# Half of the feature-spreading DMAs of a linear-attention stage issued by GpSimd instead of SyncE, with the output-bias adds queued behind them

## The chip, the cores and the metric

The kernel runs on one core of a Trainium2 chip. Its engines are TensorE (PE), VectorE (DVE), ScalarE (ACT), GpSimd (POOL) and SyncE (SP); each works through a queue of its own in order, and they meet only at semaphores. The metric is the device time of one execution in microseconds. A change of 0.2% is 4.6 us here.

## The reference

Two transformer layers in a row over 2048 tokens of width 512. The change sits in the attention of the first one, a linear attention that mixes only the 16 heads of a token with one another:

```python
q = (x @ Wq.T + bq); k = (x @ Wk.T + bk); v = (x @ Wv.T + bv)      # 16, 8, 8 heads of 32
q, k = rope(q), rope(k)
qp = sin_cos(q / |q| @ R.T);  kp = sin_cos(k / |k| @ R.T)           # 32 features per head
kv  = einsum('bhsf,bhsd->bsfd', kp, v)                              # per token, over heads
out = einsum('bhsf,bsfd->bhsd', qp, kv)
x = x + out @ Wo.T + bo
```

Before and after it stand routed spline layers, and behind those the second layer: a gated feed-forward, a differential attention and another feed-forward.

## The kernel before

Everything is written by hand, with one semaphore for each kind of step. The 2048 tokens are four chunks of 512. The attention stage runs from 230 to 705 us of the profiled execution as five rounds, `i` = -1, 0, 1, 2, 3. In round `i` each engine works on several chunks at once: `new` = i + 1 is projected and turned into features, `now` = i gets its scores, its weighted sums and its output product, `look` = i + 2 is prepared, and `back` = i - 1 is routed for the next layer. The order of each engine's queue is the order in which `b_tensor`, `b_scalar`, `b_vector`, `b_pool` and `b_sync` write it.

The features of `new` leave VectorE as six blocks `f_hi`/`f_lo` of [128, 512] in 16 bits: two of keys, then four of queries. VectorE writes the last piece of block z at L1647, semaphore `b_f_lo`. A block holds its heads along the partitions; the score product wants a head's high and low parts stacked in 96 partitions. So the blocks are copied within SBUF by DMAs, three batches for each chunk: the **keys** into `ks` once two blocks stand, the **first queries** into `qs` once four stand, the **second queries** once all six stand. Each batch is 12 DMAs, three parts by four quarters `j` of the partitions, each 32 partitions by two rows of 512, 64 KB. All are issued on SyncE's queue, `spread` at L1568. Between the first and the second queries that queue also writes the values to HBM and reads them back rearranged (L1580, one DMA; L1584, eight DMAs that wait until the write has landed).

Who waits for them: ScalarE regroups the keys at L1486 (`keys`, first in the queue ahead of the rest of the features' turns) and waits for `b_ks`; TensorE's first score product of the next round, L1298, waits for `b_qs`, that is for all 24 query DMAs:

```python
pe.wait_ge(s["b_qs"], 384 * (now + 1))     # L1289, at y == 0 of a round
e.wait_ge(s["b_ks"], 192 * (new + 1))      # L1485, ahead of keys(0)
```

GpSimd has two jobs in a round. It multiplies by the cosines (L1547) and squares (L1550) for the six blocks of `new`; and it adds the output bias to the four tiles of `now` (L1555), each as soon as VectorE has added the product to the residual (L1655, `b_res`). The statistics that VectorE takes of these tiles at step 2 of the next round (L377) wait for `b_bo`.

Of the kernel before, what the change touches and what calls it, by code (L numbers as in the profile page):

```python
# [28 lines left out]
NCH = NTOK // CH  # L29
# [61 lines left out]
ap_oh ap_turned ap_oht ap_rows ap_read  # L91
n_var n_ln n_std n_norm n_h n_turned n_hi n_lo
b_v_done b_v_in b_v_out b_vr b_qk_done b_qf b_cos b_rot b_rope b_sq b_nsum b_n2 b_ln b_n b_r b_proj b_p b_spread b_y
b_reduced b_feat b_f_hi b_f_lo b_ks b_ksg b_qs b_s b_mask b_pv b_ot_hi b_ot_lo b_out b_res b_bo
f_gate f_up f_th f_tmp f_prod f_hi f_lo f_down f_out
c_in c_h c_turned c_ct_hi c_ct_lo c_w_hi c_w_lo c_lam_in c_lam_dot c_lam_exp c_mask c_set c_qk_done c_qk c_qk_hi c_qk_lo c_v_done c_v_hi c_v_lo
c_score c_max c_negmax c_max_turned c_maxt c_scored c_exp c_p_hi c_p_lo c_av c_ev c_on c_u c_sq c_msum c_ms c_lnm c_rms
# [1099 lines left out]
PAIRS = CH // GROUP // 2  # L1197
# [22 lines left out]
def need(eng, sem, value):  # L1220

    if value > 0:
        eng.wait_ge(sem, value)


def b_roles(i):


    return [n if 0 <= n < NCH else None for n in (i, i + 1, i + 2, i - 1)]
# [49 lines left out]
def b_tensor(k, pe, i):  # L1279

    s = k.s
    now, new, look, back = b_roles(i)
# [4 lines left out]
    def score(y):  # L1287
        if y == 0:
            if now:  # L1289
                pe.wait_ge(s["b_res"], TPC * now)  # L1290
            pe.wait_ge(s["b_v_in"], TPC * (now + 1))
            pe.wait_ge(s["b_qs"], 384 * (now + 1))
        if y % 4 == 0:
            pe.wait_ge(s["b_ksg"], 4 * now + y // 4 + 1)
        need(pe, s["b_mask"], PAIRS * now + y - 1)
        for q in range(2):
            toks = slice((2 * y + q) * GROUP, (2 * y + q + 1) * GROUP)
            ins = pe.matmul(k.ps[:, SCORE_BANK[y % 2], 256 * q:256 * q + 256].rearrange("p (h t) -> p h t", h=16),  # L1298
                            k.ksg[0:96, 2 * y + q, :], k.qs[0:96, :, toks], start=True, stop=True)
        ins.then_inc(s["b_s"], 1)  # L1300
# [135 lines left out]
def grouped(ref):  # L1436

    return ref.rearrange("p a (h g) -> p a h g", g=32)  # L1440
# [5 lines left out]
def b_scalar(k, e, i):  # L1446

    s = k.s
    now, new, look, back = b_roles(i)
    route = 1 + NCH  # L1450

    def sums(g):
        e.wait_ge(s["b_pv"], PAIRS * now + 4 * g + 4)
        e.activation(grouped(k.ot_hi)[:, :, :, 8 * g:8 * g + 8],
                     k.ps[:, SUM_BANK, :].rearrange("p (a h g) -> p a h g", g=8, a=4),
                     ACT.Copy, scale=O_SCALE).then_inc(s["b_ot_hi"], 1)

    def projected(t):
        e.wait_ge(s["b_qk_done"], 6 * new + t + 1)
        e.activation(k.qf[:, t, :], k.ps[:, PROJ_BANK[t % 2], :], ACT.Identity, bias=k.bqk[:, ORDER[t]:ORDER[t] + 1],  # L1460
                     scale=1.0 / (W_SCALE * A_SCALE)).then_inc(s["b_qf"], 1)

    def inverse():
        e.wait_ge(s["b_n2"], new + 1)
        e.activation(k.nr[0:24, 1, :], k.nr[0:24, 0, :], ACT.Ln).then_inc(s["b_ln"], 1)
        e.wait_ge(s["b_ln"], new + 1)
        e.activation(k.nr[0:24, 1, :], k.nr[0:24, 1, :], ACT.Exp, scale=-0.5).then_inc(s["b_n"], 1)

    def turns(z):
        if new is None:  # L1470
            return
        e.wait_ge(s["b_p"], 6 * new + z + 1)
        need(e, s["b_reduced"], 6 * new + z - 1)
        e.activation(k.turns[:, z % 2, :], k.ps[:, WIDE_BANK, :], ACT.Copy).then_inc(s["b_spread"], 1)
        e.wait_ge(s["b_reduced"], 6 * new + z + 1)
        e.activation(k.ang[:, z % 2, :], k.ang[:, z % 2, :], ACT.Sin, bias=k.c["phase2pi"], scale=-float(2 * np.pi))\
            .then_inc(s["b_feat"], 1)
        e.wait_ge(s["b_feat"], 6 * new + z + 1)
        e.activation(k.f_hi[:, z, :], k.ang[:, z % 2, :], ACT.Copy, scale=A_SCALE).then_inc(s["b_f_hi"], 1)

    def keys(g):
        if new is None:
            return
        if g == 0:
            e.wait_ge(s["b_ks"], 192 * (new + 1))  # L1485
        e.activation(k.ksg[0:96, 8 * g:8 * g + 8, :].rearrange("p g (h t) -> p g h t", h=8),  # L1486
                     k.ks[0:96, :, P * g:P * g + P].rearrange("p h (g t) -> p g h t", t=GROUP), ACT.Copy)\
            .then_inc(s["b_ksg"], 1)

    if i == NCH - 1:  # L1490
        use_log(e)
    for y in range(PAIRS + 1):
        if now is not None and y and y % 4 == 0:
            sums(y // 4 - 1)
        if new is not None:
            if y in QK_AT:
                projected(QK_AT.index(y))
            if y == SPREAD_AT + 1:
                inverse()
        if look is not None and y == LOOK_START + 1:  # L1500
            apply_scalar(k, e, look, 1, LOOK_BANK)
        if back is not None:
            if y == 3:
                token_root_scalar(k, e, back, 1)
            if y == 5:
                token_root_scalar(k, e, back, 2)
            if y == 7:
                token_write_scalar(k, e, back)
        if i == NCH - 1:
            if y in (8, 9):  # L1510
                route_sign_scalar(k, e, back, route, 2 * y - 16, LAST_BANK)
                route_sign_scalar(k, e, back, route, 2 * y - 15, LAST_BANK)
            if y == 12:
                route_hot_scalar(k, e, back, route, LAST_BANK[0])

    body = back is not None and new is not None
    for z in range(4):
        turns(z)
    keys(0)
    keys(1)  # L1520
    turns(4)
    keys(2)
    keys(3)
    turns(5)
    if look is not None:
        use_log(e)
        norm_root_scalar(k, e, look)
        norm_write_scalar(k, e, look, look, k.h, range(TPC), s["n_h"])
    if body:
        for c in range(KC):  # L1530
            route_sign_scalar(k, e, back, route, c, BACK_BANK)
    if look is not None:
        for c in range(KC):
            turn_scalar(k, e, look, c, NEXT_TURN[c])
    if body:
        route_hot_scalar(k, e, back, route, BACK_BANK[0])


def b_pool(k, e, i):
    s = k.s  # L1540
    now, new, look, back = b_roles(i)
    if new is not None:
        for z in range(6):
            e.wait_ge(s["b_qf"], 6 * new + z + 1)
            if z == 0:
                need(e, s["b_proj"], 6 * new)
            e.tensor_tensor(k.qr[:, z, :], k.qf[:, z, :], k.c["cos"], ALU.mult).then_inc(s["b_cos"], 1)  # L1547
            e.wait_ge(s["b_rope"], 6 * new + z + 1)
            need(e, s["b_nsum"], 6 * new + z - 1)
            e.tensor_tensor(k.q2[:, z % 2, :], k.qr[:, z, :], k.qr[:, z, :], ALU.mult).then_inc(s["b_sq"], 1)  # L1550
    if now is not None:
        for u in range(TPC):
            e.wait_ge(s["b_res"], TPC * now + u + 1)
            xt = k.x[:, now * TPC + u, :]
            e.tensor_tensor(xt, xt, k.bo, ALU.add).then_inc(s["b_bo"], 1)  # L1555


def b_sync(k, sp, i):


    s, scratch = k.s, k.d["values"]
    f = (k.f_hi, k.f_lo)

    def spread(stack, parts, blocks, heads, sem):
        for part in range(3):
            for j in range(4):
                dst = stack[32 * part:32 * part + 32].rearrange("p (b j) t -> p j b t", j=4)[:, j, heads]
                sp.dma_start(dst, f[parts[part]][32 * j:32 * j + 32, blocks, :]).then_inc(sem, 16)  # L1568

    if i == 0:  # L1570
        sp.wait_ge(s["ug_out"], 16 * NCH)
    sp.wait_ge(s["b_f_lo"], 6 * i + 2)
    need(sp, s["b_ksg"], 4 * i)
    spread(k.ks, (0, 0, 1), slice(0, 2), slice(0, 2), s["b_ks"])
    sp.wait_ge(s["b_f_lo"], 6 * i + 4)
    need(sp, s["b_s"], PAIRS * i)
    spread(k.qs, (0, 1, 0), slice(2, 4), slice(0, 2), s["b_qs"])
    sp.wait_ge(s["b_v_in"], TPC * (i + 1))
    need(sp, s["b_vr"], 128 * i)
    sp.dma_start(scratch.rearrange("(u p) n -> p u n", p=P), k.v0).then_inc(s["b_v_out"], 16)  # L1580
    sp.wait_ge(s["b_v_out"], 16 * (i + 1))
    need(sp, s["b_pv"], PAIRS * i)
    for h in range(8):
        sp.dma_start(k.vr[GROUP * h:GROUP * h + GROUP], scratch[:, 32 * h:32 * h + 32]  # L1584
                     .rearrange("(g t) d -> t g d", t=GROUP)).then_inc(s["b_vr"], 16)
    sp.wait_ge(s["b_f_lo"], 6 * i + 6)
    spread(k.qs, (0, 1, 0), slice(4, 6), slice(2, 4), s["b_qs"])


def b_vector(k, V, i):  # L1590
# [456 lines left out]
def use_log(e):  # L2047

    e.preload_act_table_set("natural_log_exp_and_others")
# [858 lines left out]
```

## Time and profile before

| | |
|---|---|
| median of 3 runs | 2310.25 us (2309.74 to 2310.73) |
| the profiled execution | 2309.18 us |
| its span, first to last instruction | 2307.3 us |
| busy: PE, DVE, ACT, POOL | 2010.7, 1267.2, 727.0, 220.6 us |
| 16 DMA engines' mean busy share | about a fifth |

Busy times are sums over the whole span, and stages differ: in the second layer TensorE is nearly always busy, in the attention stage it waits for others now and then. What a transfer costs there is seen only from the instruction that waits for it.

### The profile page before, as it was taken

How to read it: one execution, taken by the hardware profiler on the slowest of the kernel's cores; microseconds unless marked ns; L12 is line 12 of the kernel's file. 1: busy time of each engine (PE TensorE's matmuls, PEld its weight loads, DVE VectorE, ACT ScalarE, POOL GpSimd, SP SyncE). 2: the span in 40 equal slices, each digit the busy share in tenths (PEclk: the TensorE clock that was granted, in tenths of full speed). 3: DMA queues.
4: the chain of work that ended last, by engine and by line, in shares of the span. 5: the costliest groups of instructions: out<-in, count | busy, mean ns of one | idle time of the engine just before them, and what ended most of it. 6: DMA issues, size and time to landing. Idle time of an engine off the chain costs nothing. (4 is left out here: it accounts for less than half of the span.)

```text
span 2307.3 us, 29065 instructions
## 1 busy us (share of the span) xinstructions
PE 2010.7 (87%) x11854; PEld 945.0 (41%) x11854; DVE 1267.2 (55%) x2323; ACT 727.0 (32%) x1131; POOL 220.6 (10%) x164
## 2 busy tenths in 40 slices
PE   4784868887864899999998999989998999999998
PEld 3442323333332444444443444444444444444443
DVE  5777447576566455554565356625574466623322
ACT  4562132333321222232243223522343223412211
POOL 3630201201100000001000100001000100000000
PEclk7986878878865899999999999999999999999999
DMA  7224030302123122212111111111111111132321
GB/s 257 92 74 171 0 60 13 48 19 42 37 51 120 64 93 100 93 54 73 46 56 46 56 46 46 57 55 43 41 65 37 64 47 56 56 101 101 112 102 60
DMA packets 91136, 158.71 MB, mean 69 GB/s; under 512 B 44342, under 2 KB 55932, under 8 KB 86268
## 3 DMA queue, kind: packets, MB, share of 16 engines
q1 hardware_dynamic: 91004, 156.86, 21.4%
q8 instruction: 94, 1.54, 0.3%
q14 instruction: 38, 0.31, 0.0%
HBM read 128.52 MB, written 18.87 MB: 64 GB/s over the span
## 5 line engine op out<-in xcount | busy, mean ns | idle before, releaser
L1184 PE MATMUL ps<-arena 128*128 128x512 f16 (+1 forms) x4512 | 1021.8, 382 | 19.8 <-DVE arena L1965 12.9
L1184 PEld LDWEIGHTS ps<-arena 128*128 128x128 f16 x4512 | 437.4, 99 | 544.2 <-issue 57.1
L1910 PE MATMUL ps<-arena 128*128 128x512 f16 x1536 | 349.1, 383 | 29.5 <-DVE arena L1956 16.2
L1910 PEld LDWEIGHTS ps<-arena 128*128 128x128 f16 x1536 | 147.4, 98 | 207.4 <-issue 29.4
L1965 DVE SCALAR_TENSOR_TENSOR arena<-arena,ps 128x512 f32<-128x512 f32 x128 | 87.8, 686 | 210.1 <-ACT arena L1932 209.5
L1932 ACT ACTIVATE arena<-ps,arena 128x512 f32<-128x512 f32 x128 | 87.6, 684 | 362.3 <-PE ps L1184 362.1
L2517 ACT ACTIVATE arena<-ps 128x1024 f32<-128x1024 f32 (+3 forms) x128 | 90.1, 704 | 254.6 <-PE ps L2426 254.5
L2622 DVE CAST arena<-arena 128x1024 f16<-128x1024 f32 (+3 forms) x128 | 66.2, 517 | 150.6 <-ACT arena L2517 148.6
L2588 DVE TENSOR_REDUCE arena<-ps 128x2 f32<-128x256 f32 (+3 forms) x128 | 99.5, 819 | 65.1 <-PE ps L2370 65.1
L1993 DVE SCALAR_TENSOR_TENSOR arena<-ps,arena 128x512 f32<-128x512 f32 x64 | 44.0, 687 | 139.6 <-PE ps L1910 139.4
L1974 DVE SCALAR_TENSOR_TENSOR arena<-ps,arena 128x512 f32<-128x512 f32 x128 | 95.7, 748 | 39.3 <-PE ps L1184 39.1
L2624 DVE TENSOR_TENSOR arena<-arena 128x1024 f16<-128x1024 f32 (+3 forms) x128 | 111.4, 870 | 4.4
L2568 POOL TENSOR_TENSOR arena<-arena 128x512 f16<-128x512 f32 x32 | 37.1, 1159 | 643.8 <-ACT arena L2495 643.8
L1956 DVE TENSOR_TENSOR arena<-arena 128x512 f16<-128x512 f32 x128 | 90.8, 710 | 4.0 <-ACT arena L1924 4.0
L1924 ACT ACTIVATE arena<-arena 128x512 f16<-128x512 f32 x128 | 79.7, 622 | 17.5 <-DVE arena L1974 17.5
L1599 DVE TENSOR_TENSOR arena<-ps,arena 128x256 f32<-128x256 f32 x128 | 47.9, 417 | 67.3 <-PE ps L1298 66.6
L1827 PE MATMUL ps<-arena 128*128 128x128 f32 x192 | 32.5, 325 | 54.7 <-ACT arena L2042 54.7
L2572 POOL TENSOR_TENSOR arena<-arena 128x512 f32<-128x512 f32 x16 | 19.0, 1186 | 581.5 <-DVE arena L2635 581.5
L2424 PE MATMUL ps<-arena 32*128 32x512 f16 (+3 forms) x768 | 72.9, 293 | 0.0
L731 PE MATMUL ps<-arena 128*128 128x128 f32 x240 | 45.6, 336 | 30.5 <-DVE arena L968 17.7
L2492 ACT ACTIVATE arena<-ps 128x512 f32<-128x512 f32 x32 | 19.1, 597 | 166.7 <-PE ps L1184 166.7
L1311 PE MATMUL ps<-arena 128*32 128x64 f32 x1024 | 42.0, 295 | 26.7 <-DVE arena L1607 14.0
(267 smaller groups left out, 2394.8 us busy)
## 6 DMA issues: line engine op xcount, KB each, us to landing
arena<-wug_dram SPq DMA_DIRECT2D x128, 512.0 KB, 3.3
arena<-wd_hi_dram SPq DMA_DIRECT2D x16, 1024.0 KB, 5.0
arena<-wd_lo_dram SPq DMA_DIRECT2D x16, 1024.0 KB, 7.2
arena<-arena SPq DMA_DIRECT2D x144, 64.0 KB, 2.1
wug_dram<-arena SPq DMA_DIRECT2D x4, 2048.0 KB, 15.8
arena<-_attn_hidden_states_dram SPq DMA_DIRECT2D x4, 1024.0 KB, 11.9
arena<-in_L_ffn_W_up_dram SPq DMA_DIRECT2D x8, 512.0 KB, 4.8
arena<-in_L_ffn_W_down_dram SPq DMA_DIRECT2D x4, 1024.0 KB, 7.3
```

Of the source, the lines that this page charges most:

```text
L1184: ins = pe.matmul(out, left[a](c), right[b](c), start=(at == 0), stop=(at == 3 * n - 1))
L1910: ins = pe.matmul(k.ps[:, bank, :], act[x][:, slot, cols], wd[y][:, f, :], start=(f == 0 and m == 0), stop=(f == 7 and m == 2))
L1924: e.activation(k.act_hi[:, g % ACT_SLOTS, :], k.prod[:, g % 2, :], ACT.Copy).then_inc(s["f_hi"], 1)
L1932: e.activation(k.th[:, g % 2, :], k.ps[:, GATE_BANK, :], ACT.Tanh, scale=k.wscale[:, FB + a:FB + a + 1])\
L1956: e.tensor_tensor(k.act_lo[:, g % ACT_SLOTS, :], k.prod[:, g % 2, :], k.act_hi[:, g % ACT_SLOTS, :], ALU.subtract)\
L1965: e.scalar_tensor_tensor(out=th, in0=th, scalar=1.0, in1=k.ps[:, GATE_BANK, :], op0=ALU.add, op1=ALU.mult)\
L1974: e.scalar_tensor_tensor(out=k.prod[:, g % 2, :], in0=k.ps[:, UP_HALF_BANK, :], scalar=k.wscale[:, a:a + 1], in1=th, op0=ALU.mult, op1=ALU ...
L2424: pe.matmul(k.ps[:, bank, queries], x[rows, 4 + b, keys], y[rows, b, queries], start=False, stop=False)
L2517: e.activation(k.p32[:, t % 2, :, queries], k.ps[:, 0:2, queries], ACT.Exp, scale=SCORE).then_inc(s["c_exp"], 1)
L2588: e.tensor_reduce(k.mx[:, u, 4 * b + 2 * j:4 * b + 2 * j + 2], k.ps[:, bank:bank + 2, 0:(u + 1) * P], AXX, ALU.max).then_inc(s["c_max"], 1)
L2622: e.tensor_copy(k.p_hi[:, t % 2, :, queries], k.p32[:, t % 2, :, queries]).then_inc(s["c_p_hi"], 1)
L2624: e.tensor_tensor(k.p_lo[:, t % 2, :, queries], k.p32[:, t % 2, :, queries], k.p_hi[:, t % 2, :, queries], ALU.subtract).then_inc(s["c_p_l ...
```

## The change

The loop over the four quarters is split. SyncE keeps quarters 0 and 1 of every batch, six DMAs; GpSimd issues quarters 2 and 3, six DMAs of the same shape, on semaphores of their own (`b_ks2`, `b_qs2`). On GpSimd all three batches stand behind the six cosine/square pairs of `new` and ahead of the four bias adds of `now`. TensorE and ScalarE wait for both semaphores.

```diff
+            pe.wait_ge(s["b_qs"], 192 * (now + 1))
+            pe.wait_ge(s["b_qs2"], 192 * (now + 1))
-            pe.wait_ge(s["b_qs"], 384 * (now + 1))
...
-            e.wait_ge(s["b_ks"], 192 * (new + 1))
+            e.wait_ge(s["b_ks"], 96 * (new + 1))
+            e.wait_ge(s["b_ks2"], 96 * (new + 1))
...
 # b_pool, after the six cosine/square pairs
+        b_keys_spread(k, e, new, (2, 3), "b_ks2")
+        b_first_spread(k, e, new, (2, 3), "b_qs2")
+        b_second_spread(k, e, new, (2, 3), "b_qs2")
     if now is not None:
         for u in range(TPC):
             e.wait_ge(s["b_res"], TPC * now + u + 1)
...
+def b_spread(k, e, quarters, stack, parts, blocks, heads, sem):
+    f = (k.f_hi, k.f_lo)
+    for part in range(3):
+        for j in quarters:
+            dst = stack[32 * part:32 * part + 32].rearrange("p (b j) t -> p j b t", j=4)[:, j, heads]
+            e.dma_start(dst, f[parts[part]][32 * j:32 * j + 32, blocks, :]).then_inc(sem, 16)
+
+def b_keys_spread(k, e, i, quarters, ks):
+    s = k.s
+    if i == 0:
+        e.wait_ge(s["ug_out"], 16 * NCH)
+    e.wait_ge(s["b_f_lo"], 6 * i + 2)
+    need(e, s["b_ksg"], 4 * i)
+    b_spread(k, e, quarters, k.ks, (0, 0, 1), slice(0, 2), slice(0, 2), s[ks])
...
 # b_sync
+    b_keys_spread(k, sp, i, (0, 1), "b_ks")
+    b_first_spread(k, sp, i, (0, 1), "b_qs")
...
+    b_second_spread(k, sp, i, (0, 1), "b_qs")
```

GpSimd's queue where round 0 ends and round 1 begins, with the semaphores each instruction waits for. Before: the last square of the six pairs, the four bias adds, the first pair of the next round.

```order
L1547 TENSOR_TENSOR arena<-arena 128x512 [waits b_qf]
L1550 TENSOR_TENSOR arena<-arena 128x512 [waits b_nsum,b_rope]
L1555 TENSOR_TENSOR arena<-arena 128x512 [waits b_res] x4
L1547 TENSOR_TENSOR arena<-arena 128x512 [waits b_proj,b_qf]
L1550 TENSOR_TENSOR arena<-arena 128x512 [waits b_nsum,b_rope]
```

And now, in the same place of the changed kernel (its lines are two or five further on):

```order
L1549 TENSOR_TENSOR arena<-arena 128x512 [waits b_qf]
L1552 TENSOR_TENSOR arena<-arena 128x512 [waits b_nsum,b_rope]
L1570 DMA arena<-arena 32x2x512 [waits b_ksg,b_f_lo]
L1570 DMA arena<-arena 32x2x512 x5
L1570 DMA arena<-arena 32x2x512 [waits b_s,b_f_lo]
L1570 DMA arena<-arena 32x2x512 x5
L1570 DMA arena<-arena 32x2x512 [waits b_f_lo]
L1570 DMA arena<-arena 32x2x512 x5
L1560 TENSOR_TENSOR arena<-arena 128x512 [waits b_res] x4
L1549 TENSOR_TENSOR arena<-arena 128x512 [waits b_proj,b_qf]
```

Eighteen DMAs in three waiting batches have come between the squares and the bias adds. The bias adds, and the next round's pairs behind them, can start only when the last query batch has been issued.

SyncE's queue for one chunk, before: keys, first queries, values out, values back, second queries.

```order
L1568 DMA arena<-arena 32x2x512 [waits b_ksg,b_f_lo]
L1568 DMA arena<-arena 32x2x512 x11
L1568 DMA arena<-arena 32x2x512 [waits b_s,b_f_lo]
L1568 DMA arena<-arena 32x2x512 x11
L1580 DMA values_dram<-arena 128x4x256 [waits b_vr,b_v_in]
L1584 DMA arena<-values_dram 16x32x32 [waits b_pv,b_v_out]
L1584 DMA arena<-values_dram 16x32x32 x7
L1568 DMA arena<-arena 32x2x512 [waits b_f_lo]
L1568 DMA arena<-arena 32x2x512 x11
```

And now:

```order
L1570 DMA arena<-arena 32x2x512 [waits b_ksg,b_f_lo]
L1570 DMA arena<-arena 32x2x512 x5
L1570 DMA arena<-arena 32x2x512 [waits b_s,b_f_lo]
L1570 DMA arena<-arena 32x2x512 x5
L1605 DMA values_dram<-arena 128x4x256 [waits b_vr,b_v_in]
L1609 DMA arena<-values_dram 16x32x32 [waits b_pv,b_v_out]
L1609 DMA arena<-values_dram 16x32x32 x7
L1570 DMA arena<-arena 32x2x512 [waits b_f_lo]
L1570 DMA arena<-arena 32x2x512 x5
```

Each batch has lost six of its twelve DMAs; the order and the values' trip between them are as they were.

## Rows read from the trace of the kernel before

**Rows 1.** The page: engine's busy time and share; issues of the spreading DMAs.

```profile
PE 2010.7 (87%) x11854; PEld 945.0 (41%) x11854; DVE 1267.2 (55%) x2323; ACT 727.0 (32%) x1131; POOL 220.6 (10%) x164
...
arena<-arena SPq DMA_DIRECT2D x144, 64.0 KB, 2.1
```

**Rows 2.** Windows: one round, and all after the stage (length, busy, clock, DMA share, GB/s).

```profile
324.00:430.00 106.00, 86.15 (x548) 38.73 (x546) 65.29 (x136) 31.60 (x47) 17.38 (x16) 0.85 0.20 33
...
705.00:2307.00 1602.00, 1499.35 (x8795) 684.06 (x8795) 817.20 (x1400) 480.39 (x748) 75.73 (x64) 0.97 0.19 66
```

**Rows 3.** TensorE's timeline: first score product of rounds 0, 1, 2, 3 (start, length, [idle before]).

```profile
323.84 0.58 PE L1298 MATMUL ps<-arena 96*128 96x256 f16 x2 [4.16 <-issue]
...
430.06 0.59 PE L1298 MATMUL ps<-arena 96*128 96x256 f16 x2 [4.08 <-issue]
...
542.25 0.61 PE L1298 MATMUL ps<-arena 96*128 96x256 f16 x2
...
647.76 1.01 PE L1298 MATMUL ps<-arena 96*128 96x256 f16 x4 [1.42 <-issue]
```

**Rows 4.** SyncE's timeline, its spreading and value DMAs (merged: start, length, count).

```profile
314.66 7.63 SPq L1568 DMA_DIRECT2D arena<-arena  x12
...
394.93 18.50 SPq L1568 DMA_DIRECT2D arena<-arena  x24
...
416.69 4.01 SPq L1584 DMA_DIRECT2D arena<-values_dram  x8
...
420.75 7.62 SPq L1568 DMA_DIRECT2D arena<-arena  x12
...
530.48 100.74 SPq L1568 DMA_DIRECT2D arena<-arena  x36
...
638.52 7.63 SPq L1568 DMA_DIRECT2D arena<-arena  x12
```

**Rows 5.** Line L1568 alone: ns to issue, min/median/max; who waited; time to landing.

```profile
L1568 SPq DMA_DIRECT2D arena<-arena x144: 585/597/1757, 288.7 to 645.6; - x144
...
  ACT arena L1486: 6.1, 4
...
DMA to landing us min/median/max: 2.0/2.1/4.9
```

**Rows 6.** ScalarE's timeline: regrouping of the keys, waiting for their batch, in four rounds.

```profile
298.40 2.00 ACT L1486 ACTIVATE arena<-arena 96x1024 f16<-96x1024 f16 x2 [1.42 <-DMA arena<-arena]
...
405.18 2.00 ACT L1486 ACTIVATE arena<-arena 96x1024 f16<-96x1024 f16 x2 [1.90 <-DMA arena<-arena]
...
513.97 2.00 ACT L1486 ACTIVATE arena<-arena 96x1024 f16<-96x1024 f16 x2 [0.95 <-DMA arena<-arena]
...
623.64 2.00 ACT L1486 ACTIVATE arena<-arena 96x1024 f16<-96x1024 f16 x2 [1.82 <-DMA arena<-arena]
```

**Rows 7.** VectorE's timeline: the sixth and last feature block of four chunks.

```profile
310.21 0.69 DVE L1647 SCALAR_TENSOR_TENSOR arena<-arena 128x512 f16<-128x512 f32 x1 [1.45 <-ACT arena L1479]
...
417.00 0.87 DVE L1647 SCALAR_TENSOR_TENSOR arena<-arena 128x512 f16<-128x512 f32 x1 [0.85 <-ACT arena L1479]
...
525.80 0.86 DVE L1647 SCALAR_TENSOR_TENSOR arena<-arena 128x512 f16<-128x512 f32 x1 [0.85 <-ACT arena L1479]
...
635.45 0.87 DVE L1647 SCALAR_TENSOR_TENSOR arena<-arena 128x512 f16<-128x512 f32 x1 [0.85 <-ACT arena L1479]
```

**Rows 8.** GpSimd's and VectorE's timeline: a bias add, the next round's first work, the statistics.

```profile
410.39 1.09 POOL L1555 TENSOR_TENSOR arena<-arena 128x512 f32<-128x512 f32 x1 [39.83 <-DVE arena L1655]
...
435.73 1.09 POOL L1547 TENSOR_TENSOR arena<-arena 128x512 f32<-128x512 f32 x1 [13.20 <-ACT arena L1460]
...
439.56 2.47 DVE L377 BATCH_NORM_STATS2 arena<-arena 128x6 f32<-128x512 f32 x4
```

**Rows 9.** VectorE's timeline beside the keys' batch: the short form of an elementwise step.

```profile
395.54 0.49 DVE L1639 TENSOR_SCALAR arena<-arena 128x512 f32<-128x512 f32 x1
396.06 0.69 DVE L1640 SCALAR_TENSOR_TENSOR arena<-arena 128x512 f32<-128x512 f32 x1
```

More of the change, by code:

```diff
@@ L93 @@
 b_v_done b_v_in b_v_out b_vr b_qk_done b_qf b_cos b_rot b_rope b_sq b_nsum b_n2 b_ln b_n b_r b_proj b_p b_spread b_y
-b_reduced b_feat b_f_hi b_f_lo b_ks b_ksg b_qs b_s b_mask b_pv b_ot_hi b_ot_lo b_out b_res b_bo
+b_reduced b_feat b_f_hi b_f_lo b_ks b_ks2 b_ksg b_qs b_qs2 b_s b_mask b_pv b_ot_hi b_ot_lo b_out b_res b_bo
 f_gate f_up f_th f_tmp f_prod f_hi f_lo f_down f_out
@@ L1555, in b_pool, with b_first_spread, b_second_spread @@
             e.tensor_tensor(xt, xt, k.bo, ALU.add).then_inc(s["b_bo"], 1)
+def b_spread(k, e, quarters, stack, parts, blocks, heads, sem):
[11 more added lines that the diff above has]
+    b_spread(k, e, quarters, k.ks, (0, 0, 1), slice(0, 2), slice(0, 2), s[ks])
+def b_first_spread(k, e, i, quarters, qs):
+    s = k.s
+    e.wait_ge(s["b_f_lo"], 6 * i + 4)
+    need(e, s["b_s"], PAIRS * i)
+    b_spread(k, e, quarters, k.qs, (0, 1, 0), slice(2, 4), slice(0, 2), s[qs])
+def b_second_spread(k, e, i, quarters, qs):
+    e.wait_ge(k.s["b_f_lo"], 6 * i + 6)
+    b_spread(k, e, quarters, k.qs, (0, 1, 0), slice(4, 6), slice(2, 4), k.s[qs])
 def b_sync(k, sp, i):
     s, scratch = k.s, k.d["values"]
[L1562 to L1577, printed above, removed]
+    b_keys_spread(k, sp, i, (0, 1), "b_ks")
+    b_first_spread(k, sp, i, (0, 1), "b_qs")
     sp.wait_ge(s["b_v_in"], TPC * (i + 1))
@@ L1585, in b_sync @@
                      .rearrange("(g t) d -> t g d", t=GROUP)).then_inc(s["b_vr"], 16)
-    sp.wait_ge(s["b_f_lo"], 6 * i + 6)
-    spread(k.qs, (0, 1, 0), slice(4, 6), slice(2, 4), s["b_qs"])
+    b_second_spread(k, sp, i, (0, 1), "b_qs")
 def b_vector(k, V, i):
```

## The prediction

> **What bounds the kernel now.** The page first: TensorE is busy for 2010.7 of 2307.3 us [rows 1]. The windows say where it is not: after 705 us it works 1499 of 1602 us and nothing is changed there; in the attention stage a round such as 324 to 430 us has it busy for 86 of 106 us, and no other engine reaches that [rows 2]. So a round is a chain over several engines, and what counts is who waits last where two rounds meet. In TensorE's timeline the first score product of round 0 comes after 4.16 us of idling, that of round 1 after 4.08, of round 2 after none, of round 3 after 1.42; "issue" is printed because no engine released it [rows 3]. SyncE's timeline names the releaser: its last query batch begins at 314.66, 420.75, 530.48 and 638.52 us, is issued in 7.63 us, and 1.5 to 1.8 us after its end TensorE starts in rounds 0, 1 and 3 [rows 3, 4]. (In round 2 it is issued by 538.1 and TensorE has routing work until 542.25.) The data was ready before that: the sixth block is finished at 310.90, 417.87, 526.66 and 636.32 us (start plus length of the rows), so SyncE begins the batch 3.76, 2.88, 3.82 and 2.20 us late, since it is still reading the values back [rows 4, 7]. Earlier in the round ScalarE waits for the keys' batch: 1.42, 1.90, 0.95 and 1.82 us, 6.1 together [rows 5, 6]. Behind this regrouping stand the turns of blocks 4 and 5, so what ScalarE loses there arrives at the sixth block, at the normalisation and at TensorE.
>
> A batch is thus mostly issue time: twelve times 0.636 us, against 2.1 us from one DMA's issue to its landing [rows 4, 5].
>
> **The change, step by step.** Each batch becomes two halves issued side by side. SyncE's takes six times 0.636, 3.8 us, half the time. GpSimd's takes six times its own price x, which the trace does not show: no DMA of before is issued there. The bounds are SyncE's median of 0.60 us from below and its longest, 1.76 us, from above [rows 5]. The nearest row of the engine itself is one of its instructions on 128x512 elements, 1.09 us [rows 8]; I take x = 1.09, hence 6.54 us for a half batch, and the same landing time as SyncE's. Against the 7.63 us of before each batch is complete s = 7.63 - 6.54 = 1.09 us sooner, relative to its start.
>
> Keys: GpSimd is idle when two blocks stand (in round 1's turn it idled 39.8 us until its bias add at 410.39 [rows 8], 15 us after the batch's start), so its half starts when SyncE's does. ScalarE gains the smaller of s and its wait: 1.09, 1.09, 0.95, 1.09 us in the four rounds. Call it d. The sixth block and everything that TensorE waits for move forward by d.
>
> Second queries: GpSimd has nothing to do with the values, so its half starts when the sixth block stands, 3.76, 2.88, 3.82 or 2.20 us (the lag) sooner than SyncE did. SyncE's own half is no later: for round 1 the values' reads, which ended at about 420.7 [rows 4], end 3.8 us sooner at 416.9, and its six are out by 420.7, before GpSimd's at 416.8 + 6.5 = 423.3. TensorE gains d plus the smaller of its idle time and lag + s:
> round 0: 1.09 + min(4.16, 4.85) = 5.25; round 1: 1.09 + min(4.08, 3.97) = 5.06; round 2: 0.95 + 0 = 0.95; round 3: 1.09 + min(1.42, 3.29) = 2.51.
> The sum is 13.8 us. The first queries, half a round ahead of their reader, cost nothing.
>
> Bias adds: four times 1.09, 4.4 us, which began at 410.4 us, now stand behind the last batch. In round 1's turn they run from 423.3 to 427.7 us. Their reader, the statistics, would start at 439.56 - 5.1 = 434.5, and GpSimd's next cosine product at 435.73 - 5.1 = 430.7 [rows 8]: costed at nothing, with 3.0 us of cover. That cover does not shrink with x, because the next round cannot start either before GpSimd's batch has landed; without it the adds would cost what they overrun, at most 4.4 us in each of two turns. One small thing goes with them: the sixth block takes 0.87 us where a bias add runs beside it and 0.69 in the chunk that has none [rows 7]; 0.2 us in the lag of three rounds, left out.
>
> At both ends of x: at 0.60 every wait is used up, 5.58 + 5.98 + 0.95 + 3.24 = 15.8 us gained. At 1.76 a half batch takes 10.5 us, s = -2.9, and the sums are -2.1, -2.9, -2.9, -3.6: 11.5 us lost. In between the gain falls to 8.1 at x = 1.27 (s = 0), 4.6 at 1.37, nothing at 1.48, and 4.6 are lost at 1.59. So x decides, with 32 to 42 us per us.
>
> The profiled execution took 2309.18 us for a span of 2307.3, and lies 1.1 us under the median of 2310.25. 2309.18 - 13.8 = 2295.4 for an execution like it; around the median that is 2296.5.
>
> **Rivals.** *No gain, because the transfers share their engines.* What the rows show of moving data: 64 KB land 2.1 us after issue while the DMA engines are busy a fifth of the time [rows 2, 5], so the batch's length is issue. Were it movement, two queues would give what one gave: no change, 2310. The Trainium skill, DMA: Bandwidth & Descriptors, section Issuing engines are not separate DMA queues, speaks against the change: all queues run on the same 16 DMA engines, and a second issuer saves only the sequencer's issue time, "usually small relative to the DMA itself". By that rule the gain would be nothing; here the issue is 7.6 us and the rest 2, which the trace shows and the rule excepts. 3 in 100.
>
> *VectorE holds GpSimd up while it writes descriptors.* VectorE has a short form, 0.49 us against 0.69 for the same 512 elements, twice beside each keys' batch and not beside the second queries [rows 9]; and the 0.87 of the bias adds' neighbour shows that the two engines can get in each other's way [rows 7]. If GpSimd's issue stands still for 2 x 0.49 = 0.98 us, d falls to 0.11: 4.27 + 4.08 + 0.11 + 1.53 = 10.0 us, 2300.3. The rule is in the Trainium skill, SBUF — State Buffer, under SBUF: two separate sides: in its two-port modes VectorE locks GpSimd out of the port by which it writes descriptors. No DMA of before is issued on GpSimd, so no run here shows it yet. 17 in 100.
>
> *GpSimd issues too slowly: slower than before.* One mechanism, at the keys and again at the second queries: over x = 1.48 the half batch on GpSimd ends later than the whole one did on SyncE, lag and all, and over 1.59 the loss is above 4.6 us. At the upper bound the time is 2321.8. For it: GpSimd takes 1.09 us for simple arithmetic and here has 64 rows of 1 KB to describe in each DMA. Against it: a DMA reads no data through the engine. 20 in 100; for a price between 1.37 and 1.59, within 4.6 us of before, 12 in 100.
>
> The Trainium skill, DMA: Bandwidth & Descriptors, section Latency and other measured facts, gives the first byte of such a DMA as about 1 us after issue against 0.6 on SyncE. By these 0.4 us s would be 0.69 and the gain 11.8 us.
>
> **How the numbers follow.** The forecast, x up to about 1.25 and nothing else in the way, has 48 in 100; its own range is 2294.5 to 2301.5. With the port lock's 17 that makes 0.65 for faster by over 0.2% (4.6 us, about what a measurement of this kernel can tell); 0.12 and 0.03 for no difference; 0.20 for slower. The range runs from 2293.5 (everything gained and 1 us of scatter) to 2313 (x = 1.55), leaving out the slower rival.
>
> **What would show it.** Right: GpSimd's batches of six take 6.5 us; ScalarE's regrouping of the keys waits 0 to 0.8 us; the first score product waits not at all or a few tenths in rounds 0 and 1; bias adds end before the next cosine product; after 705 us everything is as before, only earlier. Wrong: a GpSimd DMA over 1.4 us, or key waits longer than before; a landing much later than 2 us after GpSimd's issue; VectorE's 0.49 us steps stretched or GpSimd's issues uneven beside them; or the statistics of the next round waiting for the bias adds. A gain well above 15.8 us would mean that TensorE's clock, 0.85 in a round [rows 2], rose as well, from which I take nothing.

## The result, and the profile after

The changed kernel takes 2294.3 us (median of 4, 2293.97 to 2296.02) against 2310.02 for the kernel before (median of 4 on the same chip): a ratio of 0.9934, 95% interval 0.9922 to 0.9947, faster by 15.7 us. The prediction was 2296.5. Two later measurements of the changed kernel gave 2295.0 and 2295.5, gains of some 15.2 us over the kernel before beside them. The traced executions differ by less, 2294.2 for 2307.3 us of span: the old one's trace is of a run somewhat below its median, and the changed one's is of the slowest of its four.

The page of the changed kernel, to be held against [rows 1], and its window from 705 us on, against [rows 2]:

```profile
span 2294.2 us, 29080 instructions
...
PE 2006.6 (87%) x11854; PEld 944.4 (41%) x11854; DVE 1268.6 (55%) x2323; ACT 726.7 (32%) x1131; POOL 258.7 (11%) x236
...
arena<-arena SPq DMA_DIRECT2D x72, 64.0 KB, 2.9
arena<-arena POOLq DMA_DIRECT2D x72, 64.0 KB, 2.7
```

```profile
705.00:2294.00 1589.00, 1491.61 (x8774) 678.57 (x8772) 809.37 (x1368) 474.63 (x738) 75.73 (x64) 0.98 0.19 67
```

GpSimd has 72 instructions and 38 us more, the price of issuing; no engine has fewer instructions. VectorE's last L543 step of the attention stage, before and after:

```profile
703.99 1.02 DVE L543 TENSOR_REDUCE arena<-arena 128x128 f32<-128x512 f32 x1
...
691.11 1.02 DVE L543 TENSOR_REDUCE arena<-arena 128x128 f32<-128x512 f32 x1
```

From there to the end of the span are 1603.3 and 1603.1 us: behind the stage nothing has changed but the time at which it happens. Counted to this step from one of VectorE's early in the stage (L1776, at 284.68 us in the old trace), the stage takes 419.3 us before and 406.0 after. Below, "the stage" is this stretch. Unlike the bare time of a row it does not depend on how late a trace comes into the stage, which differs by up to 2.3 us between the traces here.

The price itself stands in the view of the spreading line (ns to issue: min/median/max):

```profile
L1570 SPq DMA_DIRECT2D arena<-arena x72: 585/597/1509, 289.2 to 627.9; - x72
L1570 POOL DMA_DIRECT2D arena<-arena x72: 533/533/702, 289.8 to 627.5; - x72
```

GpSimd issues in 0.533 us, less than SyncE, and less than the lower bound that I had set. Its timeline in the turn of round 1, and SyncE's in that of round 0, first before (two lines) and then after:

```profile
389.53 3.21 POOL L1570 DMA_DIRECT2D arena<-arena  x6 [25.07 <-DVE arena L1671]
400.01 3.17 POOL L1570 DMA_DIRECT2D arena<-arena  x6 [7.28 <-DVE arena L1671]
410.15 3.16 POOL L1570 DMA_DIRECT2D arena<-arena  x6 [6.96 <-DVE arena L1671]
```

```profile
307.37 0.59 SPq L1580 DMA_DIRECT2D values_dram<-arena  x1
310.59 4.03 SPq L1584 DMA_DIRECT2D arena<-values_dram  x8
...
304.21 0.58 SPq L1605 DMA_DIRECT2D values_dram<-arena  x1
307.42 4.03 SPq L1609 DMA_DIRECT2D arena<-values_dram  x8
311.49 3.79 SPq L1570 DMA_DIRECT2D arena<-arena  x6
```

On GpSimd each batch waits for nothing but VectorE's block, and takes 3.2 us. On SyncE the values leave at 304.21, where they left at 307.37 before, because the first queries ahead of them are six DMAs and not twelve. TensorE's first score products, against [rows 3]:

```profile
319.12 0.38 PE L1299 MATMUL ps<-arena 96*128 96x256 f16 x2 [0.56 <-DMA arena<-arena]
319.97 2.77 PE L1184 MATMUL ps<-arena 128*128 128x512 f16 x12 [0.47 <-DVE arena L1866]
...
418.22 0.60 PE L1299 MATMUL ps<-arena 96*128 96x256 f16 x2
419.80 4.91 PE L1184 MATMUL ps<-arena 128*128 128x512 f16 x12 [0.99 <-DVE arena L1866]
...
531.89 0.61 PE L1299 MATMUL ps<-arena 96*128 96x256 f16 x2
...
633.23 1.01 PE L1299 MATMUL ps<-arena 96*128 96x256 f16 x4
```

They come 4.7, 11.8, 10.4 and 14.5 us earlier than in [rows 3]; the prediction's sums up to these places were 5.3, 10.3, 11.3 and 13.8. The waits of 4.16 and 4.08 us are gone, and those of ScalarE in [rows 6] too, all four. What TensorE waits for now is the next line: the projection right behind the scores needs what VectorE makes at L1866, one of the turns ahead of it. So the score is no longer the last wait of a turn, and its time flatters the change: the projection behind it stands at 319.97, 419.80 and 532.29 us where it stood at 324.22, 430.44 and 542.65, and the first weighted sum of round 3 at 636.44 where it stood at 649.28. That is 4.3, 10.6, 10.4 and 12.8 us.

Two things in the trace were in no term. The first is the clock. Of the 14.5 us, some come from matmuls that run at the higher of two levels. The projection behind the first score of round 0 takes 2.77 us for its 12 matmuls, before 4.68. In round 3 a row of 24 takes 5.34 us, before 7.03; the windows of the two stretches read 1.00 and 0.76, and shortly before them TensorE was idle for 0.98 us in the new kernel and 2.90 in the old, waiting for ScalarE, which in the old one had waited for the keys. It does not go one way only: the projections of rounds 1 and 2 take 4.91 and 4.99 us, before 4.48 and 4.69. The rows before, and the window of the stretch in round 3, before and after:

```profile
324.22 4.68 PE L1184 MATMUL ps<-arena 128*128 128x512 f16 x12
628.19 7.03 PE L1184 MATMUL ps<-arena 128*128 128x512 f16 x24
```

```profile
628.20:635.20 7.00, 7.00 (x27) 2.93 (x26) 3.90 (x6) 4.86 (x7) 1.61 (x2) 0.76 0.42 122
...
616.40:621.70 5.30, 5.30 (x27) 2.48 (x26) 2.63 (x5) 3.70 (x5) 0.00 (x0) 1.00 0.50 159
```

The second is a loss. In round 3 the four bias adds stand in a heap behind the last batch, and beside them VectorE's product for the routing takes 2.79 us where it took 0.69:

```profile
628.04 4.23 POOL L1560 TENSOR_TENSOR arena<-arena 128x512 f32<-128x512 f32 x4
```

```profile
630.04 2.79 DVE L522 TENSOR_TENSOR arena<-arena 128x512 f32<-128x512 f32 x1
```

```profile
636.44 0.67 PE L1312 MATMUL ps<-arena 128*32 128x64 f32 x16 [2.20 <-DVE arena L1623]
```

TensorE waits 2.20 us for what VectorE does next; before it was 0.5. The old trace has the effect too, where one multiplication of GpSimd's stands beside the same step:

```profile
548.15 1.09 POOL L1547 TENSOR_TENSOR arena<-arena 128x512 f32<-128x512 f32 x1 [16.82 <-ACT arena L1460]
```

```profile
548.28 1.51 DVE L522 TENSOR_TENSOR arena<-arena 128x512 f32<-128x512 f32 x1
```

### The profile page after: what moved, and what is told of

The parts are those of the page before. It is cut to its first block and busy times, and to the rows that moved or that the text cites. A ratio compares the mean times of both kernels' runs of the same rounds, so it can differ in the third digit from the quotient of the medians.

```text
span 2294.2 us, 29080 instructions
## 1 busy us (share of the span) xinstructions
PE 2006.6 (87%) x11854; PEld 944.4 (41%) x11854; DVE 1268.6 (55%) x2323; ACT 726.7 (32%) x1131; POOL 258.7 (11%) x236
## 5 line engine op out<-in xcount | busy, mean ns | idle before, releaser
L1312 PE MATMUL ps<-arena 128*32 128x64 f32 x1024 | 42.1, 294 | 28.5 <-DVE arena L1623 14.5
## 6 DMA issues: line engine op xcount, KB each, us to landing
arena<-_attn_hidden_states_dram SPq DMA_DIRECT2D x4, 1024.0 KB, 11.8
```

## The experiments

Twelve measurements of ten kernels, in three groups, each with runs of the kernel before beside it: the first is e0 to e3 (2310.27 us before), the second e4 to e7 (2310.36), the third e8 to e11 (2310.68). The last column is how much shorter the stage is in the kernel's one trace than the 419.3 us of before; it is 13.3 in the first trace of the changed kernel. `all` in the diffs is `(0, 1, 2, 3)`, all four quarters; the counts in the waits go with it.

| kernel | GpSimd issues | us | ratio, 95% | stage, us less |
|---|---|---|---|---|
| e0_again | as changed | 2295.0 | 0.9931 (0.9918 to 0.9945) | 13.4 |
| e11_again | as changed | 2295.5 | 0.9935 (0.9922 to 0.9947) | 13.4 |
| e1_keys | half of keys | 2309.6 | 0.9998 (0.9989 to 1.0007) | 0.0 |
| e8_first | half of first queries | 2299.2 | 0.9952 (0.9940 to 0.9965) | 9.8 |
| e2_second | half of second queries | 2306.9 | 0.9986 (0.9977 to 0.9995) | 2.3 |
| e9_keys_first | halves of keys and first | 2299.1 | 0.9953 (0.9940 to 0.9967) | 10.2 |
| e3_all | all of all three | 2304.4 | 0.9977 (0.9968 to 0.9986) | 6.8 |
| e4_values | the values instead | 2317.4 | 1.0031 (1.0018 to 1.0043) | -11.2 |
| e5_fill1 | as changed, 2 for 1 | 2298.4 | 0.9957 (0.9941 to 0.9973) | 9.0 |
| e6_fill2 | as changed, 3 for 1 | 2323.8 | 1.0060 (1.0046 to 1.0073) | -14.2 |
| e7_bias2 | as changed, 2 adds earlier | 2295.7 | 0.9936 (0.9924 to 0.9949) | 16.6 |
| e10_bias2_again | the same | 2291.3 | 0.9923 (0.9910 to 0.9935) | 16.7 |

**The changed kernel again** (no edit), twice.

> The changed kernel once more. In its first profile the span was 13.1 us shorter than before, by the medians of unprofiled runs it was 15.7. Theory 'waits': the gain is the waits removed at the four turns, the rest is the clock of TensorE falling differently from one execution to the next; then the median repeats at 2294 to 2295, the gain at each turn's first projection repeats within 0.3 us (4.7, 5.2, 1.0 us in rounds 0 to 2), and the missing 2 us move about inside the rounds. Theory 'scatter': 15.7 was a lucky set; then the median is nearer 2297.

> The changed kernel itself beside the other three on the same chip: a median of 2294 to 2295 us, as in both measurements of it before.

The first median is as expected, the second is 0.5 us above. The first projections of rounds 0 to 2 stand within 0.1 us of where the first trace has them once each trace is counted from the start of the stage. The traces have 13.3 to 13.4 us, the medians 15.2 to 15.7: some 2 us of the medians' gain are in no trace.

**One batch at a time: keys, then second queries.**

```diff
 # e1_keys: b_pool
-        b_first_spread(k, e, new, (2, 3), "b_qs2")
-        b_second_spread(k, e, new, (2, 3), "b_qs2")
 # e2_second: b_pool
-        b_keys_spread(k, e, new, (2, 3), "b_ks2")
-        b_first_spread(k, e, new, (2, 3), "b_qs2")
 # b_sync, for what GpSimd has lost: (0, 1) becomes all
```

> GpSimd issues its half of the keys' batch only; both query batches are whole on SyncE. Theory 'two terms' (each turn gives the keys' wait d plus the smaller of TensorE's idle time and lag + s): ScalarE's waits of 1.42, 1.90, 0.95 and 1.82 us vanish, but TensorE still waits for a query batch that SyncE starts after first queries and values, at a time that the keys do not move; only round 2, where no batch is waited for, gains: 0.95 us, about 2309. Rival 'the keys' wait shifts everything behind it': 6.1 us, 2304.

> GpSimd issues its half of the second queries only; keys and first queries are whole on SyncE. Theory 'two terms', with SyncE's half now the later one (values read until 314.66 or 420.75, six DMAs in 3.8 us) and the turns' outputs as the cap: 3.2 + 3.1 + 0 + 1.4 = 7.7 us, 2302.3; with this and the keys alone at 1, the parts sum to under 9 and the whole gives 15. Rival 'parts add up': the keys alone and this one sum to the 15.7 of the whole, so about 10 here if the keys give 6.

Keys alone: nothing; the 0.7 us of the medians are not told from none, and the stage has 0.0. ScalarE waits no longer, and TensorE gets to its first score sooner, only to wait there 6.09 us instead of 4.16. Its timeline:

```profile
323.49 0.59 PE L1298 MATMUL ps<-arena 96*128 96x256 f16 x2 [6.09 <-issue]
```

SyncE had read the values back from 310.25 to 314.28 and issued the last batch from 314.31 on, as before: a block that is ready sooner is no help when the queue is late. Second queries alone: 3.4 us, not the 7.7 that were expected. SyncE and the issues of the spread batch (the page's landing times) in e2_second:

```profile
311.78 4.55 SPq L1606 DMA_DIRECT2D arena<-values_dram  x8
316.38 4.66 SPq L1567 DMA_DIRECT2D arena<-arena  x6
```

```profile
arena<-arena POOLq DMA_DIRECT2D x24, 64.0 KB, 5.5
```

GpSimd's half is early, but SyncE's half still stands behind the values, and ends at 321.0 where the whole batch had ended at 322.3 (2.5 us sooner, since this trace comes into the stage 1.3 us later than the old one). Besides, GpSimd's six fall on the values' reads: they land after 5.5 us, and the reads after 5.1 instead of 4.0, so the two slow each other down when they run together. In the whole change the reads are over by 311.45, one microsecond after GpSimd begins.

Neither part, nor their sum, makes the gain of the whole change. That left the batch that the prediction had costed at nothing.

**The first queries' half alone, and with the keys'.**

```diff
 # e8_first: b_pool
-        b_keys_spread(k, e, new, (2, 3), "b_ks2")
-        b_second_spread(k, e, new, (2, 3), "b_qs2")
 # e9_keys_first: b_pool
-        b_second_spread(k, e, new, (2, 3), "b_qs2")
 # b_sync, for what GpSimd has lost: (0, 1) becomes all
```

> GpSimd issues only its half of the first queries; keys and second queries are whole on SyncE. Theory of SyncE's queue: halving this batch lets SyncE write and read back the values 3.8 us sooner, so the whole second query batch starts sooner by the lag at most (3.76, 2.88, 3.82, 2.20 us), and the first score moves by the least of that, 3.8, and what TensorE had to wait beyond VectorE's turn (3.18, 3.10, 0, 1.42): 3.2 + 2.9 + 0 + 1.4 = 7.5 us, 2302.8. SyncE's last batch starts about 311, 418, 527 and 636 us in the old kernel's times. Rival, the prediction's own step that the first queries' batch costs nothing: no change, 2310.4. If keys' half alone (0.65 us measured) and second half alone (3.4) were all there is, the whole change could not give 15.

> GpSimd issues its halves of keys and first queries; second queries whole on SyncE. Theory of SyncE's queue: the 7.5 us of the first queries' half, and the keys' 1.0 to 1.9 us a round no longer swallowed by the queue except where it is bound: some 11 us in all, 2299. Rival (each half's gain stands by itself): 7.5 + 0.65 = 8.2 us, 2302.2; by the prediction's terms alone, keys only, 2309.7.

The first queries' half alone gives 11.5 us, three quarters of the whole (9.8 of 13.4 in the stage). SyncE in e8_first:

```profile
303.42 0.59 SPq L1602 DMA_DIRECT2D values_dram<-arena  x1
306.90 4.03 SPq L1606 DMA_DIRECT2D arena<-values_dram  x8
310.97 7.63 SPq L1567 DMA_DIRECT2D arena<-arena  x12
```

```profile
320.16 0.59 PE L1299 MATMUL ps<-arena 96*128 96x256 f16 x2 [0.67 <-issue]
```

The last batch is whole, 7.63 us long, but starts 3.7 us sooner (310.97 for 314.66), and TensorE's first score comes 3.7 us sooner. The queue theory said 7.5 us and 11.5 were measured; its trace has 8.3 up to the first score of round 3 (639.46 for 647.76), 9.8 by the end of the stage and 10.4 in the whole span. So the theory is right in kind and nearly in size up to that score; what gives the rest is open. Its other claim, that the keys' half gains another 3.5 us once the queue is shorter, failed: e9_keys_first is no faster. In its round 0 the reads start at 307.18 and the score waits 2.14 us, the queue's end again, as in e1_keys. In round 1 part of the keys' gain is lost at VectorE, whose fifth block takes 2.23 us for 0.69 beside a bias add; and the queue binds again, since the sixth block stands at 413.80 and SyncE starts the last batch at 415.06, behind the values. How much goes to which is not separated.

```profile
407.66 1.10 POOL L1559 TENSOR_TENSOR arena<-arena 128x512 f32<-128x512 f32 x1
```

```profile
407.09 2.23 DVE L1670 SCALAR_TENSOR_TENSOR arena<-arena 128x512 f16<-128x512 f32 x1 [0.85 <-ACT arena L1480]
```

With the second queries' half added, 3.6 us come on top, from e9_keys_first to the changed kernel beside it (2299.1 to 2295.5; 3.2 in the stage): it halves the batch behind the values, and it moves the adds away from the fifth and sixth blocks, which take 0.69 us each in the changed kernel. The two were not tried apart.

**GpSimd issues all twelve of each batch.**

```diff
 # b_pool: (2, 3) becomes all, three times; b_sync:
-    b_keys_spread(k, sp, i, (0, 1), "b_ks")
-    b_first_spread(k, sp, i, (0, 1), "b_qs")
-    b_second_spread(k, sp, i, (0, 1), "b_qs")
```

> GpSimd issues all twelve DMAs of every batch, SyncE none but the values. GpSimd took 0.53 us for one, so a whole batch takes 6.4 us against 7.6 on SyncE and s is 1.2. Theory 'what counts is a queue that the values do not hold up': 1.2 + 3.2, 1.2 + 3.1, 0.95, 1.2 + 1.4 = 11.3 us, less up to 2 us in round 3 for VectorE held up by bias adds: 2299 to 2301. Rival 'what counts is two issuers side by side': nearly nothing is gained, 2308 to 2310.

2304.4, between the two. The price is 0.53 us here too, and twelve take 6.3 us, but the third batch starts late:

```profile
301.04 6.34 POOL L1568 DMA_DIRECT2D arena<-arena  x12 [4.18 <-DVE arena L1666]
314.42 6.31 POOL L1568 DMA_DIRECT2D arena<-arena  x12 [7.04 <-issue]
```

No engine released it: "issue" again, and the sixth block had stood since 310.74. The next kernels show the same pause closer up.

**The price raised:** behind each of GpSimd's spreading DMAs one or two more of 64 rows each (768 B a row), to an unused place in HBM; GpSimd waits for their landing once, behind the stage.

```diff
             e.dma_start(dst, f[parts[part]][32 * j:32 * j + 32, blocks, :]).then_inc(sem, 16)
+            if sem is k.s["b_ks2"] or sem is k.s["b_qs2"]:
+                for _ in range(1):     # 2 in e6_fill2
+                    e.dma_start(k.d["fill"][k.filled]...).then_inc(k.s["b_fill"], 16)
```

> The changed kernel, but GpSimd issues after each of its spreading DMAs one more of 32 by two runs of 768 bytes from the constants to HBM, whose data nobody reads: the price x of a DMA on its queue doubles to about 1.07 us, which is the price that the prediction assumed. By its sum 13.8 us less than before; with the turns' outputs as caps (3.2 and 3.1 us) 4.3 + 4.2 + 0.95 + 2.5 = 11.9, 2298. Rival 'GpSimd's price hardly matters, its data come early enough anyway': 2294 to 2295 as without the fillers.

> Two fillers after each: x about 1.6 us. The prediction's sum turns at 1.48 and gives 5 us slower than before at 1.6 (s = -2.0): 2315. Rival 'the batch on GpSimd can be late without harm, since SyncE's half and other waits cover it': not slower than before.

With x doubled to 1.07, nearly the 1.09 of the prediction, the median is 2298.4. That does not confirm the 2296.5 which the prediction gave for such a price: it is the middle of four runs in two pairs, 2293.1 and 2294.4, 2302.4 and 2303.0, and the trace is of the fastest. In it the stage is 9.0 us shorter, where the prediction's formula gives some 14. The other 8 us of this run lie behind the stage, where the kernel is unchanged:

```profile
695.99 1.02 DVE L543 TENSOR_REDUCE arena<-arena 128x128 f32<-128x512 f32 x1
```

From this step to the end are 1595.2 us; in every other trace of this document there are 1602.7 to 1603.4. Its clock there stands at the higher level where the others' falls now and then: for 955 to 985 us the windows read 1.00, and 0.94 in the changed kernel. Why, no run shows.

With x at 1.6 it is 13.5 us slower than before, where the formula gives 5; its four runs lie within 2.6 us. Both traces show more than price. GpSimd in e5_fill1, in the second and third batch of a chunk:

```profile
306.48 0.54 POOL L1570 DMA_DIRECT2D arena<-arena  x1
309.44 0.53 POOL L1573 DMA_DIRECT2D fill_dram<-arena  x1 [2.42 <-issue]
...
315.41 0.54 POOL L1573 DMA_DIRECT2D fill_dram<-arena  x1
319.73 0.53 POOL L1570 DMA_DIRECT2D arena<-arena  x1 [3.79 <-issue]
```

The first batch of twelve goes out without a pause; then GpSimd stands still for 2.4 us ahead of the twelfth DMA of the second batch, and for 3.8 ahead of the eleventh of the third. Every later batch of this trace has a pause at its eleventh or twelfth too, of 1.0 to 4.0 us. The changed kernel, with six at a time and 7 us between them, hardly gets there; its only pause is of 0.25 us, in round 3. So e5_fill1 and e6_fill2 hold the pauses besides the raised price, and are no clean test of x in the formula.

**The values on GpSimd, all spreads on SyncE.**

```diff
 # b_pool
-        b_keys_spread(k, e, new, (2, 3), "b_ks2")
-        b_first_spread(k, e, new, (2, 3), "b_qs2")
-        b_second_spread(k, e, new, (2, 3), "b_qs2")
+        b_values(k, e, new)      # the nine DMAs of the values, as they were
```

> All spreading DMAs are whole on SyncE as before; the values' trip (one DMA out, a wait for it, eight DMAs back of 16 partitions by 32 runs of 128 bytes each) is on GpSimd, ahead of the bias adds. It takes the lag away and leaves the issue time. Theory 'two terms' with s = 0 and no keys' gain: min(3.2, 3.8) + min(3.1, 2.9) + 0 + 1.4 = 7.5 us, 2302.5, if GpSimd issues a DMA of 512 runs as fast as one of 64 (0.53 us). If its price goes by the runs (8 x 0.53 = 4.3 us each, 34 us for eight), the values come late for the first weighted sum and the bias adds behind them late for the statistics: 5 to 30 us slower than before. The rival 'the halves' issue time is all' expects no change, 2310.

The first half of the theory holds: SyncE now issues its 36 DMAs in a row, and in round 0 TensorE waits 0.47 us for the score where it had waited 4.16. That is the second kernel, beside e8_first, in which the lag goes once SyncE's queue is rid of what held it up:

```profile
321.14 0.58 PE L1298 MATMUL ps<-arena 96*128 96x256 f16 x2 [0.47 <-issue]
```

Yet it is 7 us slower (six runs from 2312.8 to 2321.0), as expected for late values: TensorE's weighted sums wait 10.7 us for them in three places. But they are not late by the expected mechanism. Issuing a DMA of 512 short runs takes 0.64 us, hardly more than 0.53 for 64 rows, so the price is not by runs; what grows is the pause, before every one of them but the first of each eight:

```profile
311.80 0.64 POOL L1602 DMA_DIRECT2D arena<-values_dram  x1 [2.54 <-issue]
315.44 0.63 POOL L1602 DMA_DIRECT2D arena<-values_dram  x1 [3.00 <-issue]
```

DMAs of 512 runs pause at each, DMAs of 64 rows in e5_fill1 at every eleventh or twelfth. A fixed room for descriptors, some 700 rows of it, comes to mind. But in e3_all, also in batches of twelve, the first 24 DMAs of a chunk go out with no pause among them in three of four chunks; and a DMA lands 2 to 3 us after its issue by the median, while the pauses come some 6 us into a batch, so it is not simply what is in flight. What makes GpSimd pause is open; no kernel here changed such a room.

**Two bias adds ahead of the second queries, two behind**, against the heap in round 3.

```diff
+        if now is not None:
+            for u in range(0, 2):
+                e.wait_ge(s["b_res"], TPC * now + u + 1)
+                ...                                  # the add
         b_second_spread(k, e, new, (2, 3), "b_qs2")
```

> The changed kernel with the first two of the four bias adds between first and second queries on GpSimd, the other two behind. In round 3's turn the changed kernel shows one VectorE step (L522) of 2.79 us instead of 0.69 while four bias adds run back to back. Theory 'the adds hold VectorE up and the mask behind it': that step falls to about 0.7, and the kernel is 1.5 to 2 us faster than the changed one, 2292.5 to 2293. Rival 'covered': no difference, 2294.3. The two adds beside the sixth block may cost 0.2 us in its place.

> The kernel with two bias adds ahead of the second queries once more, beside the changed kernel on the same chip. Its trace has 2.0 us less at the first weighted sums of round 3 (VectorE's product 0.90 us, not 2.79), so theory: 1.5 to 2 us faster than the changed kernel of the same call. Rival: given back before the end, same time within 0.7 us.

In the trace of e7_bias2 the heap's price is gone: VectorE's product takes 0.90 us, and TensorE's wait is 0.51 again.

```profile
634.60 0.67 PE L1312 MATMUL ps<-arena 128*32 128x64 f32 x16 [0.51 <-DVE arena L1633]
```

The medians don't settle what it is worth: 2295.7 in one group, where the changed kernel had 2295.0 in another, then 2291.3 beside 2295.5. The first says no gain, the second 4.2 us, more than the 2.0 of the mechanism; the ranges overlap in both. The traces say more: the stage is 16.6 and 16.7 us shorter than before in the two of this kernel, and 13.3 to 13.4 in the three of the changed one. So the stall's removal is shown, and a stage shorter by 3.3 us in the traced executions; a faster kernel by the medians is not.

## Why the prediction was right, and where it was wrong

**The time** was 2.2 us too high, and the chain that it read was the true one: the second query batch is what TensorE waits for at the turn, and its lag behind the sixth block is the time to be had.

**Who gives the lag back: this step failed.** "The first queries, half a round ahead of their reader, cost nothing", said the prediction, and booked the lag to GpSimd's starting at the sixth block. Alone, the half of the first queries gives 11.5 us, that of the second queries 3.4, that of the keys 0.7, which may be none. The lag is made on SyncE's queue, in which the first queries stand ahead of the values and the values ahead of the second queries; six DMAs fewer in front free it 3.7 us sooner in e8_first (310.97 for 314.66). The prediction had this very shift in a subordinate clause (SyncE's reads "end 3.8 us sooner"), as a reason why SyncE's half is not in the way, and did not see that the shift alone gives most of the gain.

**The keys' term, d = 1.09 us a round,** was sound as a movement of the sixth block and wrong as time: taken alone it became a longer wait at the first score (6.09 us). With the first queries' half it adds 0.4 us to the stage and nothing to the median; it can count only where the queue behind is short, as with the second queries' half. The keys' share in the whole change was not measured by itself.

**x, mis-sized:** 0.533 us for 1.09. By the formula everything is then used up and 15.8 us gained; 15.7 were measured. That agreement is luck: the stage has 13.3 to 13.4 us in three traces. In the old trace the turn's output stands at 321.04 and 427.34 us, 3.2 and 3.1 us ahead of the first projection, so about 1 us of each wait in rounds 0 and 1 could not be won by any batch; the heap took another 1.7 in round 3; and the clock gave part of it back, 1.9 and 1.7 us in the rows shown less 0.4 and 0.3 in the projections of rounds 1 and 2. "From which I take nothing" was an omission of the size of a term. At the price that the prediction assumed, its 13.8 us are not borne out either: e5_fill1 has 9.0 in the stage, with pauses in them. (One sum of the prediction is off by a rounding: at s = 0.69 its formula gives 11.9 us, not 11.8.)

**The rivals.** The shared engines give no ban, but a grain of truth: landing rose from 2.1 to 2.9 us on SyncE, and to 5.5 in e2_second, where the batch met the values' reads. The first byte that was to come later from GpSimd does not show: 2.7 us to landing there, 2.9 on SyncE. The port lock on descriptors does not show either: in the changed kernel VectorE's 0.49 us steps stand beside GpSimd's batches, and the longest of 72 issues is 0.70 us. "GpSimd issues too slowly" did not come true at 0.533 us; e6_fill2, at x = 1.6, is a kernel where it does, and its loss of 13.5 us for the formula's 5 comes with the pauses, which the formula did not have.

**The bias adds** "costed at nothing, with 3.0 us of cover": the cover against their reader held (the adds end at 417.56, and the statistics begin at 429.33), but they are not free for the neighbour. The prediction asked who waits for them and not who works beside them; [rows 7] had shown 0.87 for 0.69, the same trace has 1.51 at 548.28 us, and a heap of four made that 2.79.

## What to carry to other kernels

When a queue issues several things in a row, a wait at its end is paid by everything ahead on the queue: price an instruction by what stands behind it there, not by how far off its own reader is. Moving half the issues to an idle engine pays where a batch is mostly issue time; keep the bursts on GpSimd short (of six DMAs with 7 us between, all but one were free of pauses here; of twelve, with 4 us or less between, many were not), and out of step with other small transfers. Before letting postponed GpSimd arithmetic pile up, look at what VectorE does in the stretch where the pile will run.

## What the runs showed of the hardware

- GpSimd issues a DMA of 64 rows of 1 KB in 0.533 us and one of 512 runs of 128 bytes in 0.64; SyncE takes 0.60 for the first.
- GpSimd pauses in long rows of such DMAs: 1.0 to 4.0 us at the eleventh or twelfth of every batch but the first in e5_fill1, and ahead of the third batch of twelve in three of the four chunks of e3_all; and at each DMA of 512 runs but the first of eight (2.5 to 3.6 us, e4_values). The cause was not tested.
- Six 64 KB copies within SBUF that meet eight reads of 128-byte runs land after 5.5 us instead of 2.0 to 2.7, and the reads after 5.1 instead of 4.0.
- A VectorE step with two inputs in SBUF took 2.79 us for 0.69 beside four GpSimd adds of 1.06 us each, back to back. The Trainium skill, SBUF — State Buffer, Who interferes with whom, has a VectorE instruction with two inputs in SBUF contend with a GpSimd instruction that reads SBUF, for one shared pair of ports that whoever issues first holds for its whole instruction. The traces agree: in the stage of five of them (before, changed, e7, e9, e10), each such step that is stretched beside a GpSimd add or multiplication ends 0.54 to 0.56 us after that instruction, be it 0.87 us long, 1.51 or 2.79, the last after the fourth add of the heap. In e9_keys_first the step is printed as starting 0.57 us ahead of the add, and ends at the same distance behind it, so the rule's order does not show there; GpSimd's starts in the profile are rough.
